# A gate activation placed ahead of a softmax exponential in a macaron block (chunked attention between two half-step FFNs)

## The reference, cut to what matters

```python
x = x + 0.5 * ffn(layernorm(x))            # ffn: one 1024 x 1024 matrix built from small factors, + bias
x = x + attn(layernorm(x))
x = x + 0.5 * ffn(layernorm(x))

def attn(x):                               # 16 heads of 64, chunks of 64 tokens, 32 chunks
    q, k, v = split(x @ W_qkv)
    p = softmax(mask(q @ k.T * SCALE))     # causal, inside each chunk only
    out_local = p @ v
    cum_k, cum_v = sums over the earlier chunks of the chunk means of k and v
    cross = sigmoid(q . cum_k * SCALE)     # one gate per token and head
    return (out_local + 0.5 * cross * cum_v) @ W_out
```

## Time and profile before

| What | Value |
|---|---|
| median of 9 runs | 662.52 us (659.57 to 687.29) |
| the profiled execution, its own time | 660.87 us |
| span of its slowest core (core 5), first to last instruction | 659.0 us |
| spans of the eight cores | 647.9 to 659.0 us |
| PE busy | 433.3 us, 66% of the span |
| DVE busy | 391.5 us, 59% |
| ACT busy | 189.5 us, 29% |
| attention rounds in the span | about 213 to 523 us, eight of some 39 us |

### The profile page before, as it was taken

One profiled execution on the slowest core, in us unless ns is written; L12 is line 12 of the kernel. 1 busy time (PEld: TensorE's weight loads), 2 busy tenths in 40 slices (PEclk: granted clock), 3 DMA queues, 4 the chain that ended last, 5 costly groups with the idle time before them and its releaser, 6 DMA issues.

```text
span 659.0 us, 8519 instructions; the slowest of 8 cores (647.9 to 659.0 us)
## 1 busy us (share of the span) xinstructions
PE 433.3 (66%) x3120; PEld 232.5 (35%) x3120; DVE 391.5 (59%) x681; ACT 189.5 (29%) x169; POOL 22.9 (3%) x26
## 2 busy tenths in 40 slices
PE   0000006878604959779596877959688499959996
PEld 0000002333201544636355463634546244423442
DVE  0299989888881263533726344371624658778775
ACT  0000000000011564737567374755737300010000
POOL 5000000000000000000000000010000000000000
PEclk9999999999956878969698895969879589987999
DMA  8920007870048040400404031066000192009834
GB/s 194 285 98 0 0 0 139 141 72 1 0 93 163 1 49 1 44 6 2 49 0 49 1 35 16 2 66 111 2 0 2 24 188 46 0 13 184 266 145 161
DMA packets 98955, 43.61 MB, mean 66 GB/s; under 512 B 93441, under 2 KB 93569, under 8 KB 98914
## 3 DMA queue, kind: packets, MB, share of 16 engines
q1 hardware_dynamic: 72002, 33.57, 21.0%
q0 software_dynamic: 26912, 9.49, 13.1%
HBM read 26.78 MB, written 8.39 MB: 53 GB/s over the span
## 4 chain that ended last, share of the span: by engine, by line
PE 50%; DVE 25%; issue 10%; ACT 8%; DMA 5%; SPq 2%; DVEq 1%; POOL 0%; ACTq 0%; POOLq 0%
PE PSQ L435 10%; PE PB L478 9%; PE PW L435 9%; PE PW L334 8%; PE PW L335 8%; DVE ln_tm L199 5%; DMA ln_tm<-g2i 4%; DVE bnst L184 3%; DVE x_tm L353 3%; DVE vt L350 3%; DVE bnst L185 3%; ACT ptm L594 2%; ACT L594 2%; PE PB L676 2%; ACT L633 2%
## 5 line engine op out<-in xcount | busy, mean ns | idle before, releaser
L334 PE MATMUL PW<-wffn,ln_fm 128*128 128x512 bf16 x256 | 100.2, 391 | 27.9 <-DVE ln_tm L199 15.4
L335 PE MATMUL PW<-wffn,ln_fm 128*128 128x512 bf16 x256 | 100.2, 391 | 0.0
L435 PE MATMUL PSQ<-ln_fm,wqkv_j 128*128 128x512 bf16 x256 | 73.7, 453 | 22.9 <-DMA ln_fm<-ln_tm 22.9
L193 ACT ACT_TABLE_LOAD x3 | 3.8, 1283 | 253.4 <-DVE mv L187 155.2
L447 ACT ACT_TABLE_LOAD x32 | 41.1, 1283 | 115.5 <-PE PSQ L435 89.8
L456 DVE TENSOR_REDUCE chk<-kf 128x32 f32<-128x2048 bf16 x8 | 18.3, 2286 | 88.5 <-ACT kf L447 88.5
L260 PE MATMUL PW<-b,ones_s 1*128 1x512 bf16 x2 | 1.2, 605 | 98.3 <-DVE cumk L252 98.3
L435 PE MATMUL PW<-ln_fm,wqkv_j 128*128 128x512 bf16 x256 | 60.2, 390 | 4.9 <-DMA ln_fm<-ln_tm 4.9
L478 PE MATMUL PB<-wqkv_j,ln_fm 128*128 128x128 bf16 x1024 | 58.6, 219 | 0.0
L478 PEld LDWEIGHTS PB<-wqkv_j,ln_fm 128*128 128x128 bf16 x1024 | 57.2, 98 | 3.3 <-issue 3.3
L494 DVE CAST vt<-PB 128x512 bf16<-128x512 f32 x32 | 22.2, 694 | 59.3 <-PE PB L478 59.3
(11 more groups left out here) (88 smaller groups left out, 565.7 us busy)
## 6 DMA issues: line engine op xcount, KB each, us to landing
x_tm<-x_in SPq DMA_DIRECT2D x4, 2048.0 KB, 37.2
y_out<-x_tm SPq DMA_DIRECT2D x16, 512.0 KB
wqkv_j<-w_qkv POOLq DMA_DIRECT2D x8, 768.0 KB, 8.2
wout_sb<-w_out POOLq DMA_DIRECT2D x1, 2048.0 KB, 13.7
ln_fm<-ln_tm SPq DMA_TRANSPOSE x64, 3.3
ln_tm<-g1r POOLq DMA_DIRECT2D x1, 256.0 KB, 9.5
ln_tm<-g1i POOLq DMA_DIRECT2D x1, 256.0 KB, 11.3
gm_s<-gm POOLq DMA_DIRECT2D x1, 256.0 KB, 18.1
```

The lines of the kernel that those rows point to most:

```text
L334: te.matmul(ps[:, 0:512], lhsT, wmat[:, f, 0:512], start=first, stop=last)
L335: mm = te.matmul(ps[:, 512:1024], lhsT, wmat[:, f, 512:1024], start=first, stop=last)
L435: mm = te.matmul(ps[:, half * 512:half * 512 + 512], wqkv_j[:, slot, part, f, :], ln_fm[:, f * T + tq * 512: f * T + (tq + 1) * 512], star ...
```

## The change

Two calls in the loop's list change places: the gate's post step of half 1 is emitted ahead of the softmax's post step of quarter 1.

```diff
             cumv_pe = emit_tlow(chv_dve)
             bdcv_dve = emit_bdcv(cumv_pe)
+            emit_gate_post(1)
             emit_sgrp_post(1)
-            emit_gate_post(1)
             emit_pv_group(0, bdcv_dve)
```

## The result

| | before | after |
|---|---|---|
| median | 661.6 us (33 runs) | 678.3 us (11 runs, 675.1 to 680.5) |
| ratio after / before | | 1.0259 (95% interval 1.0237 to 1.0281) |
| profiled execution, its span on core 5 | 660.87, 659.0 us | 679.4, 677.6 us |

The change makes the kernel 2.6% slower, some 17 us; 676 us were forecast.

The account below looks back on a forecast made before the run. Each attention round's tail was bound by ACT (exp1 with its load, then tanh1), then quarter 0 on PE, with the clock slowing the heads after. 660.87 + 12.6 (late recip0) + 2.7 (heads) = 676.2 us; range 670 to 681.

Parts of the forecast that it names:

- tanh1 does not start earlier: On ACT, tanh1 still waits until msig0 has read `tanh_sb`; its load begins at 314.75 instead of 314.77, gaining 0.02 us a round.
- the way back: Hand-over between ACT and DVE, measured from tanh1's end to msig1's start: 0.10 us, taken for msig0 to tanh1.
- exp1 one load and one activation later, mask1 ahead of recip0: exp1 ends 4.65 us later on ACT; on DVE mask1 waits for it, so recip0 starts 1.44 us later in j=2.
- the direct term: Delays of recip0 on DVE over eight rounds, 3 x 1.44, 1.54 and 4 x 1.68 us: together 12.6 us.
- Nothing regained on the way: From recip0 through exp3, mask3 and recip2 to the next head, the whole delay stays; only recip1 has slack.
- The heads: 16 matmuls on PE after each tail: 5.8 us for all seven, 40.6 in all, 2.7 us more than before.
- The sum: Whole kernel: profiled execution 660.87 us plus 12.6 of delays ahead of recip0 plus 2.7 of heads, 676.2 us.
- Rival 1: On ACT, tanh1 does not wait for msig0: about 659 us, no change or barely faster; chance 0.04.
- Rival 2: On ACT, one table load serves two activations, so a load is saved: about 663 us; chance 0.03.
- Rival 3: On PE, every head shrinks to 4.56 us as the clock gives the delay back: about 667 us; chance 0.12.

Follow-up runs that it names:

- The run with two buffers: Changed kernel with a second buffer for the tanh (`tanh_sb`), so that tanh1 no longer waits for msig0: 660.8 us, 0.9959 of before.
- ACT's half alone: Against the kernel before, tanh1 ahead of exp1 on ACT, while DVE keeps mask1 ahead of msig1: ratio 1.0277, 679 us.
- the early scores: Against the kernel before, quarter 1's scores inside the v phase, half 1's gate in PSQ, masks and msig0 moved earlier: 650.3 us, ratio 0.9857.
- DVE's half: Against the kernel before, msig1 ahead of mask1 on DVE, while ACT keeps exp1 ahead of tanh1: 663.3 us, ratio 1.0036.
- the third kernel with the longer tail: Against the kernel before, tanh1 ahead of exp1 on ACT only, plus an unread DVE sum of some 0.6 us ahead of recip0: 687.6 us, 1.0432.

## Why the prediction was right, point by point

**tanh1 does not start earlier: right.** It starts 0.08 us behind msig0's end (320.82 to 320.90); I had taken 0.10 from the way back. The run with two buffers shows that this wait, and nothing else in the order, holds it.

**exp1 one load and one activation later, mask1 ahead of recip0: right, and 0.08 us a round short.** The 5.47 us from msig0's end to recip0 were 5.55: behind mask1 recip0 starts after 0.72 us (325.65 to 326.37), not the 0.61 that I read off mask2 and recip1. Over eight rounds the direct term is 12.6 + 0.6 = 13.2 us.

**Nothing regained on the way: right.** exp3's load follows recip0 by 3.09 us (326.37 to 329.46) and recip2 that by 3.03 (329.46 to 332.49), both as before. recip1 used up its slack, 2.54 us behind recip0 instead of 3.58, and it helped nothing.

**The heads: right in kind, a little too large.** All settle at one size, as forecast, and at 5.7 instead of 5.8 us. The first three are shorter, 5.44 to 5.65, since the settling takes some rounds: what is missing to 5.73 halves from round to round (0.29, 0.15, 0.08 us), as it must where a head grows by half the time at the 1.2 GHz level and the clock comes back at equal distances. Their sum over seven rounds is 39.5 us, 1.7 more than before; I had put 2.7.

**The sum.** On the core whose rows I used, 13.2 + 1.7 = 14.9 us, against my 12.6 + 2.7 = 15.3: two misses of opposite sign that partly cancel. From the load ahead of round 0's second copy to the last exponential the timelines of ACT give, first of before and then of after:

```profile
218.83 1.28 ACT L447 ACT_TABLE_LOAD   x1 [8.47 <-PE PW L435]
...
517.62 1.02 ACT L594 ACTIVATE ptm<-PW 128x1024 bf16<-128x1024 f32 x1
```

```profile
221.73 1.28 ACT L447 ACT_TABLE_LOAD   x1 [8.40 <-PE PW L435]
...
535.39 1.02 ACT L594 ACTIVATE ptm<-PW 128x1024 bf16<-128x1024 f32 x1
```

These are 298.79 and 313.66 us, 14.87 more. The remaining 3.7 us of the span's 18.6 lie outside the attention: 2.9 ahead of it, where the cores differ by more than that in either kernel (this load starts at 208.5 to 218.8 us before and at 210.1 to 221.7 after), and 0.8 behind it. Over all eight cores the same stretch is 297.0 to 298.9 us before and 313.6 to 315.0 after, in the mean 16.3 us more. The delays ahead of recip0 make 13.3 us of that and the heads 3.0: the other cores' heads were shorter than core 5's before, by 0.8 us in the mean, and are longer after, by as much, since on four cores of the changed kernel they come down to 5.7 us from 6.1. So the sum of 15.3 us was 1 us short of the mean core. What else separates my 676 us from 678 lies outside the attention, in the mean 0.9 us ahead of it and 0.5 behind, for which the sum had no term and the runs show no cause.

**The rivals.** Rival 1 (tanh1 does not wait) did not happen; as an experiment it gave its 659 us within the interval. Rival 2 (a load saved) did not happen: 80 loads, as before. Rival 3 (the clock gives the delay back) did not happen in the change, but with ACT's half alone the heads did shrink to 4.6 us, which hid 1.1 us a round.

## What to carry to other kernels

Before moving an instruction ahead of its neighbour on one engine, look at what it waits for: exp1 cost nothing where it stood, because tanh1 could not have run in that time. Then look at what the neighbour releases; its consumers stand in other queues, here mask1 right ahead of the step on which the next quarter hangs. A tail that lets TensorE's clock fall is paid for in steps: an added 0.6 us a round cost 2 us in one kernel and 10 us in another, so that the time of a small change to such a loop says little about the change unless the heads are read beside it.

## What the runs showed of the hardware that I had not expected

How regular the return of the clock is. Worked out from the heads as in the prediction, it comes back about 37.6, 41 or 44.3 us after its return in the round before, on every core of every trace here, whatever the tail; the head takes up the difference. From the end of a head to the start of the next it is 32.3 us with the early scores, 35.2 in the changed kernel and 36.35 with ACT's half. There one of the distances leaves a head of a size that occurs, and the rounds settle at 37.54, 40.95 and 40.99 us. It is 33.5 or 33.7 us before the change, 34.1 with DVE's half and 37.0 in the third kernel with the longer tail. There every distance would leave a head shorter than 4.2 us or longer than 6.8, none settles, and long and short heads alternate.

So two kernels whose tails differ by 1.1 us a round took the same time (1.0259 and 1.0277, with overlapping intervals), because the time of the head at the 1.2 GHz level shrank by twice the difference. On the slowest cores, whose rows stand here, no head with all its 16 matmuls on record was shorter than 4.54 us or longer than 6.20, against 3.45 us at the 2.4 GHz level; the 4.3 us in one of my expectations was a head with a record missing.
